# Shared expert in a two-layer block: tails of gate and up in one stationary block, a stacked down tail, and an earlier gather of the first rows

## What is computed

```
x = x + tanh(g_xattn[0]) * conv_attention(ctx, ctx, layernorm(x))        # the conv stage
x = x + tanh(g_ffn[0])   * moe(layernorm(x))                             # shared and routed experts
x = x + tanh(g_xattn[1]) * linear_attention(layernorm(x), ctx)
x = x + tanh(g_ffn[1])   * soft_moe(x)

def moe(x):
    topk_w, topk_idx = top_k(softmax(x @ router_w.T), 2)                 # weights sum to 1
    shared = (silu(x @ s_gate_w + s_gate_b) * (x @ s_up_w + s_up_b)) @ s_down_w + s_down_b
    return shared + sum over the chosen experts of weight * expert(x)
```

## Time and profile before

| what | us |
|---|---|
| median of three runs (1761.22 to 1765.13) | 1762.69 |
| the profiled execution | 1761.46 |
| its span, from the first to the last instruction | 1759.6 |
| PE busy in the span | 1572.1 (89%) |
| PE busy from 350 to 400 us, of 50 | 49.90 |
| mean granted clock of PE, as a share of 2.4 GHz | 0.954 |

### The profile page before, as it was taken

How to read it: one execution, slowest core, us unless ns; L and a number is a source line. 1 busy time by engine, 2 the same in 40 slices (tenths; PEclk the granted TensorE clock), 3 DMA queues, 4 the chain that set the end, 5 groups by cost and what they waited for, 6 DMA issues and landing times. The chain is left out here.

```text
span 1759.6 us, 27544 instructions
## 1 busy us (share of the span) xinstructions
PE 1572.1 (89%) x9484; PEld 913.1 (52%) x9484; DVE 1091.7 (62%) x2221; ACT 756.3 (43%) x1392; POOL 512.9 (29%) x428
## 2 busy tenths in 40 slices
PE   4989948999799999879888887889999999999997
PEld 3778833444356566435344443545555555555554
DVE  7998845335623343368586874766676767575663
ACT  5443214333123333234343452656564656566462
POOL 0657824333324444234342331120202010111101
PEclk7999979999999999889899998989999999999998
DMA  9545544745596898552425226624160505142241
GB/s 208 140 118 155 161 143 137 202 145 154 169 213 177 220 221 198 206 197 84 144 84 168 66 77 239 199 61 92 41 132 6 125 18 113 41 90 60 61 91 42
DMA packets 293579, 228.83 MB, mean 130 GB/s; under 512 B 197778, under 2 KB 241298, under 8 KB 291170
## 3 DMA queue, kind: packets, MB, share of 16 engines
q1 hardware_dynamic: 244912, 156.73, 34.7%
q10 hardware_dynamic: 39298, 40.54, 7.9%
q0 software_dynamic: 9264, 30.15, 5.6%
HBM read 125.58 MB, written 54.87 MB: 103 GB/s over the span
## 5 line engine op out<-in xcount | busy, mean ns | idle before, releaser
L2136 POOL TENSOR_TENSOR s_h_lo<-s_h,s_h_hi 128x512 f16<-128x512 f32 x32 | 36.9, 1154 | 552.8 <-DVE s_h_hi L2338 552.8
L1275 DVE TENSOR_TENSOR e_h<-e_up,e_silu 128x352 f32<-128x352 f32 x39 | 20.4, 524 | 138.7 <-ACT e_silu L1220 123.5
L2356 PE MATMUL s_ring<-w_mu,s_xt_hi 128*128 128x512 f16 x256 | 98.5, 385 | 5.9 <-DMA w_mu<-mu_split 2.8
L2264 DVE TENSOR_REDUCE s_top<-s_lg 128x1 f32<-128x512 f32 x64 | 43.9, 686 | 93.4 <-ACT s_lg L2178 93.2
L2357 PE MATMUL s_ring<-w_mu,s_xt_hi 128*128 128x512 f16 x256 | 98.5, 385 | 0.0
L2358 PE MATMUL s_ring<-w_mu,s_xt_lo 128*128 128x512 f16 x256 | 98.2, 384 | 0.0
L2356 PE MATMUL s_acc<-w_w,s_g_hi 128*128 128x512 f16 x256 | 97.1, 379 | 0.1
L524 PE MATMUL ring<-prod_hi,toep 128*128 128x288 f16 x320 | 92.8, 290 | 4.9 <-DVE terms L438 4.7
L2356 PE MATMUL s_ring<-w_w,s_xt_hi 128*128 128x512 f16 x256 | 97.0, 379 | 0.0
L2357 PE MATMUL s_ring<-w_w,s_xt_hi 128*128 128x512 f16 x256 | 97.0, 379 | 0.0
L2358 PE MATMUL s_ring<-w_w,s_xt_lo 128*128 128x512 f16 x256 | 97.0, 379 | 0.0
(11 more groups left out here) (387 smaller groups left out, 4793.7 us busy)
## 6 DMA issues: line engine op xcount, KB each, us to landing
expert_rows<-e_y SPq DMA_DIRECT2D x39, 256.0 KB
a_part_in<-in_L_ffn_W ACTq DMA_DIRECT2D x32, 256.0 KB
w_split<-a_part_q ACTq DMA_DIRECT2D x32, 256.0 KB
w_w<-w_split SPq DMA_DIRECT2D x8, 1024.0 KB, 21.6
toep<-ssm_split ACTq DMA_DIRECT2D x14, 512.0 KB, 5.3
stage<-in_L_ffn_gate_w SPq DMA_DIRECT2D x8, 704.0 KB
stage<-in_L_ffn_up_w SPq DMA_DIRECT2D x8, 704.0 KB
xattn_w_split<-e_part_q ACTq DMA_DIRECT2D x20, 256.0 KB
```

The lines of the kernel that those rows point to most:

```text
L2264: V.tensor_reduce(top[:, t, j:j + 1], lg[:, t, j * D:(j + 1) * D], AX.X, ALU.max).then_inc(S["top_done"], 1)
L2356: mm(out_, a[0], b_[0], start=first, stop=False)
```

## The change

- In the conv stage the normalised rows live in `rows_ahead` instead of `xq`. Ahead of the last store, when all earlier stores have landed, SP gathers partitions 0 to 119 of chunk 0's x1 rows from DRAM into `rows_ahead`; behind the store it copies the last 8 partitions from `gated`, in four transfers, and the block's end waits for them. The first normalisation reads `rows_ahead`; the load of chunk 0's x1 into the shared phase stays, for the residual, but stands behind the up pieces.
- The host gives gate without its last 64 columns, and in front of up a block of 128: the last 64 of gate, the last 64 of up. One block of 12 matmuls then gives gate's tail on partitions 0 to 63 and up's on 64 to 127 of one bank. Silu reads the lower half and writes the upper, and h of the tail stands on the upper half.
- The last 64 rows of down are loaded twice, to both halves of the partitions. POOL writes the tail's `h_lo` to the lower half of `h_hi`'s tail. One matmul over 128 rows then makes hi*hi + lo*hi, a second over the upper 64 rows hi*lo.
- The two up pieces have homes of their own (the buffer of silu and h, and the one of `xq`), so that four pieces are issued without a wait. ACT and DVE split the gate pieces ahead of the turned rows, the up pieces after them.

```diff
@@ conv_stage, SP
             for s in range(STEPS):
+                if s == STEPS - 1:
+                    sp.wait_ge(turned["q"], 8)
+                    for u in range(2):
+                        sp.wait_ge(stored[u], (STEPS - 1 - u) // 2 * 16 + (0 if u else 16))
+                    first = P - SSM_I
+                    sp.dma_start(k.ahead.home[0:first, :, :], x1_rows[0:first]).then_inc(k.ahead.x1_loaded, 16)
                 store(s)
+                if s == STEPS - 1:
+                    for t in range(4):
+                        sp.dma_start(k.ahead.home[first:P, t, :], gated[t:P:2 * B, s % 2, :]).then_inc(k.ahead.x1_last, 16)
...
+            sp.wait_ge(k.ahead.x1_last, 4 * 16)
@@ shared_phase, SP
-            load_x(0, 0)
...
             for n, piece in enumerate(pieces):
-                if n >= 2:
-                    sp.wait_ge(sw_lo, n + 1)
-                sp.dma_start(staged(piece, n % 2), piece[2]).then_inc(stage_loaded[n % 2], 16)
+                if n == 4:
+                    load_x(0, 0)
+                if n >= 4:
+                    sp.wait_ge(sw_lo, n - 1 if n < 6 else n + 1)
+                if n == NP - 1:
+                    for half in (LOW, HIGH):
+                        sp.dma_start(staged(piece, n)[half], piece[2]).then_inc(piece_loaded(n)[0], 16)
+                    continue
+                sp.dma_start(staged(piece, n), piece[2]).then_inc(piece_loaded(n)[0], 16)
@@ ACT (DVE likewise with rest_of_turned)
-            split_turned(0)
             for n, piece in enumerate(pieces):
+                if n == 2:
+                    split_turned(0)
@@ POOL
-                    nc.gpsimd.tensor_tensor(h_lo[0:r, m, :], h[0:r, u, :], h_hi[0:r, m, :], ALU.subtract).then_inc(h_lo_done, 1)
+                    nc.gpsimd.tensor_tensor((h_lo[:, m, :] if m < SK - 1 else h_hi[LOW, m, :]), h[r, u, :], h_hi[r, m, :], ALU.subtract).then_inc(h_lo_done, 1)
@@ PE
-                    for o, (hi, lo) in enumerate(((sg_hi, sg_lo), (su_hi, su_lo))):
+                    for o, (hi, lo, at) in enumerate((gate_, up_) if m < SK - 1 else (both,)):
+                        cols = slice(at, at + P)
...
-                        nc.tensor.matmul(tr[:, t, :], h_hi[0:r, m, tok], sd_hi[0:r, m, :], start=(m == 0), stop=False)
-                        nc.tensor.matmul(tr[:, t, :], h_hi[0:r, m, tok], sd_lo[0:r, m, :], start=False, stop=False)
-                        last = nc.tensor.matmul(tr[:, t, :], h_lo[0:r, m, tok], sd_hi[0:r, m, :], start=False, stop=(m == SK - 1))
+                        nc.tensor.matmul(tr[:, t, :], h_hi[:, m, tok], sd_hi[:, m, :], start=(m == 0), stop=False)
+                        last = nc.tensor.matmul(tr[:, t, :], h_hi[r, m, tok], sd_lo[r, m, :], start=False, stop=(m == SK - 1))
+                        if m < SK - 1:
+                            nc.tensor.matmul(tr[:, t, :], h_lo[:, m, tok], sd_hi[:, m, :], start=False, stop=False)
```

More of the change, by code:

```diff
@@ L151, in conv_stage @@
         rows = {"c": sb("c_rows", [P, B, D]), "q": sb("x_rows", [P, B, D])}
-        xn = sb("xq", [P, 4, D])
+        xn = k.ahead.home
         ssm, d_col = sb("ssm", [SSM_H, PAD]), sb("d_col", [SSM_H, 1])
@@ L583, in shared_phase @@
         taken[0] = 6656
-        sg_hi, sg_lo = (lent(KD * I_SH).rearrange("p (k i) -> p k i", k=KD) for _ in range(2))
+        sg_hi, sg_lo = (lent(KD * WHOLE).rearrange("p (k i) -> p k i", k=KD) for _ in range(2))
+        taken[0] = 6656 + 2 * KD * I_SH
         xt = lent(2 * KD * CH).rearrange("p (k i) -> p k i", k=2 * KD)
@@ L626, in shared_phase @@
         stage_loaded = [sem(f"stage_loaded{u}") for u in range(2)]
+        up_loaded = [sem(f"up_loaded{u}") for u in range(2)]
         x_loaded = [sem(f"x1_loaded{u}") for u in range(2)]
@@ L650, in shared_phase, with staged, piece_loaded @@
             e = min(b + 2, whole)
-            pieces.append((sd_hi[:, b:e, :], sd_lo[:, b:e, :], s_down[b * P:e * P, :].rearrange("(k p) n -> p k n", p=P), P))
+            pieces.append((sd_hi[:, b:e, :], sd_lo[:, b:e, :], s_down[b * P:e * P, :].rearrange("(k p) n -> p k n", p=P), slice(0, P)))
         rest_rows = I_SH - whole * P
-        pieces.append((sd_hi[0:rest_rows, whole:SK, :], sd_lo[0:rest_rows, whole:SK, :],
-                       s_down[whole * P:I_SH, :].rearrange("(k p) n -> p k n", k=1), rest_rows))
+        tail_rows = slice(0, P)
+        pieces.append((sd_hi[tail_rows, whole:SK, :], sd_lo[tail_rows, whole:SK, :],
+                       s_down[whole * P:I_SH, :].rearrange("(k p) n -> p k n", k=1), tail_rows))
         NP = len(pieces)
         assert NP % 2 == 0
-        def staged(piece, u):
+        def staged(piece, n):
             hi, _, _, rows = piece
-            k_, n = hi.shape[1], hi.shape[2]
-            return stage[0:rows, u, 0:k_ * n].rearrange("p (k n) -> p k n", n=n)
+            k_, cols = hi.shape[1], hi.shape[2]
+            home_ = {2: gated[:, :, :].rearrange("p a i -> p (a i)"), 3: xq.rearrange("p t q d -> p (t q d)").bitcast(F32)}.get(n, stage[:, n % 2, :])
+            return home_[rows, 0:k_ * cols].rearrange("p (k n) -> p k n", n=cols)
+        def piece_loaded(n):
+            return (up_loaded[n % 2], 16) if n in (2, 3) else (stage_loaded[n % 2], (n // 2 + (n < 2) + (n >= NP - 1 and n % 2)) * 16)
         def expert_weights(n):
@@ L759, in _ @@
                 for m in range(SK):
-                    r, u, n = rows_of(I_SH, m), m % 2, c * SK + m
+                    r, u, n = rows_at(m), m % 2, c * SK + m
+                    g = slice(0, r.stop - r.start)
                     act.wait_ge(gu_done, n + 1)
@@ L826, in normalise @@
             def normalise(c, u):
-                dve.wait_ge(x_loaded[u], (c // 2 + 1) * 16)
-                ln.statistics(nc, dve, x_in[u], c)
+                rows_ = x_in[u] if c else k.ahead.home
+                if c:
+                    dve.wait_ge(x_loaded[u], (c // 2 + 1) * 16)
+                else:
+                    dve.wait_ge(k.ahead.x1_loaded, 16)
+                    dve.wait_ge(k.ahead.x1_last, 4 * 16)
+                ln.statistics(nc, dve, rows_, c)
                 if c == 1:
@@ L2479, in transformer @@
         k.gates, k.tanh_gates = sb("gates", [P, 4]), sb("tanh_gates", [P, 4])
+        sb, _, sem = opener(nc, whole)
+        k.ahead = RowsAhead(sb, sem)
         down_whole, down_tail = scratch("down_whole", (P, 2, E, 2 * D), F16), scratch("down_tail", (I_MOE - 2 * P, 2, E, D), F16)
@@ L2483, in transformer @@
                    a[F + "down_w"], down_whole, down_tail)
-        sb, _, sem = opener(nc, whole)
-        k.ahead = RowsAhead(sb, sem)
         with ExitStack() as routed:
@@ L2538 @@
         a[new] = columns(a.pop(old))
+    F, whole = "L0_ffn_s_", I_SH // P * P
+    gate, up = a[F + "gate_w"], a[F + "up_w"]
+    a[F + "gate_w"] = gate[:, :whole]
+    a[F + "up_w"] = np.concatenate([gate[:, whole:], up[:, whole:], up[:, :whole]], axis=1)
+    a["s_up_b_cols"][P // 2:, SK - 1] = a["s_up_b_cols"][:P // 2, SK - 1]
     a["L1_ffn_mu"] = a["L1_ffn_mu"].reshape(D, ES)
```

54 lines of the change are left out of this document (34 added, 20 removed).

## The result

The changed kernel took 1747.62 us (median of four executions, 1746.63 to 1749.83) against 1762.76 for the kernel before on the same chip: 15.1 us less, a ratio of 0.9923 (95% interval 0.9905 to 0.9940). The forecast was 22.8 us less. The sign held, and the time lies inside the stated range (1735 to 1749), but outside the forecast's own 1736.5 to 1744: a third of the gain did not come.

A forecast was written before the change was run, and what follows sets the result against it. Bounds: a load-and-split chain at the shared expert's head, PE in the middle, DVE in the last chunk. Gains 13.5 + 0.4 + 7.1 + 1.8 = 22.8 us off 1761.46 gave 1738.7, median 1740, range 1735 to 1749.

The forecast's parts named there:

- (a): End of conv stage: early gather and four copies delay the shared phase's first load by 1.5 us, bounds 0 to 3.6.
- T: Time of SP's first load of the shared phase, 240.70 before; forecast 1.5 us later.
- (b): Head of the shared phase: new load and split order brings S 15.0 us nearer to T.
- S: Time of SP's first load of expert weights, 280.25 before (T + 39.6); forecast T + 24.6.
- chunk 0: Shared phase's first chunk, hanging on S: 0.4 us left of the shorter down product, the transposes taking the rest.
- (c): Gate and up tails in one block: 12 matmuls fewer per chunk, 2.6 us plus 0.1 for the width change.
- (d): Down product tails: two matmuls instead of three for each of four token tiles, 0.86 us a chunk.
- chunk 3: Last chunk of the shared phase: block 5's gain reaches DVE's gating product, which waited 1.82 us; 1.8 us gained.
- E: DVE's first expert product, 492.94 before; the prediction had what comes after 477 us untouched, moving as a whole.
- The chain of the head: Loads and splits of shared weights: PE's up half at T + 16.8, first expert load at T + 24.6.
- the slower rival: 64-row matmuls on the upper half stall PE at 32 changes; 1772 us at 1 us each; chance 0.03.
- the head gives only the early rows: Rival: queue holds up and down pieces back, S gains at most 6.9 less 1.5 us; time 1748; chance 0.13.

The follow-up runs named there:

- e11: The changed kernel itself, unaltered, run again on another chip for a second trace: median 1743.97 us, ratio 0.9930 to the kernel before.
- e8: Changed kernel, but all 128 partitions gathered from input x and the four copies left out; one run, no ratio, SP's first load at 243.14.
- e4: Changed kernel with chunk 0 reordered: POOL's fourth split behind the last h_lo, DVE's fourth row remainder behind block 5's gating product; ratio 0.9912 to the kernel before.
- e6: Changed kernel with PE's order changed in chunk 0's down product: blocks 0 to 3 of all token tiles first, then 4 and 5; ratio 0.9918 to the kernel before.
- e2: Changed kernel without early rows and with the head's old order, leaving only the matmul part: 1752.39 us, ratio 0.9949 to the kernel before.
- e1: Changed kernel without the early gather and copies, x1 loaded first in the shared phase: ratio 0.9922 to the kernel before.
- e3: Changed kernel with partitions 0 to 103 gathered ahead of store 14, the rest copied behind stores 14 and 15: ratio 0.9875 to the kernel before.
- e10: Changed kernel with rows gathered by step pairs, the copies' wait moved later, chunk 0's fourth POOL split and DVE remainder later: 1739.03 us, ratio 0.9892 to the kernel before.

## Why the prediction was too large, by its own steps

| step | forecast | measured |
|---|---|---|
| (a) T later | -1.5 | -6.0 |
| (b) S nearer to T | 15.0 | 14.2 |
| chunk 0 | 0.4 | -1.7 |
| (c), (d) in chunks 1 and 2 | 7.1 | 6.9 |
| chunk 3, to DVE's last operation | 1.8 | 1.5 |
| from there to E (e11: +0.7) | 0 | -0.8 |
| sum | 22.8 | 14.1 |

Each measured term is a difference of the marks above: (b) is 39.55 less 25.31, chunk 0 is 6.59 less the 8.28 by which S moved, and so on.

**The step that failed is (a)**, a term that was mis-sized: 1.5 us, bounded by 3.6, where the runs show 6.0. It had both of its parts and put them over each other: the copies as 0 to 3.6 us, and the gather, 2.6 us at 370 GB/s, which "may hold up the last store by as much; that is inside the same bounds". They are not beside each other. The store and the copies stand behind the gather in one queue, so the parts add. The gather held up the store by 4.5 us: 2.7 in the shape of e8, and 1.8 because the rate was read from transfers of 128 partitions and the one in question had 120. The copies cost 0.8, and 0.7 lie ahead of the store. That 2.6 and 3.6 make 6.2, near the 6.0, would have been luck: the gather costs more than its part and the copies less. The bounds should have taken a lower rate for a shape that no row showed. (The 2.0 us that the prediction names from the Trainium skill, DMA: Bandwidth & Descriptors, Anatomy of one DMA, stand there for transfers that POOL issues, and the copies are SP's.)

**Chunk 0 failed too**: 0.4 us forecast, 1.7 lost. I looked for what is next late among the transposes, rightly (S + 42.4 before, and e4 and e6 end on them), but not at POOL. Its split of the fourth expert piece stands between `h_lo` of blocks 3 and 4. Before, PE came to that point with waits of 1.1 and 0.7 us, and the granted clock stayed at 1.00. With 12 matmuls less in front it comes earlier and waits 3.5, and then works at half the clock. Either alone would have stayed hidden: without the waits (4.0) or without the half clock (3.0) PE would have been through by some S + 41 or S + 42 (estimates from the S + 44.6 of the changed kernel), ahead of the transposes at S + 42.3 (e6) to 43.1 (e4). Together they end 1.5 to 2.3 us behind them. e2 shows this without the rest of the change, e6 its full size.

**What held.** The chain of the head: its links came 0.2 to 1.4 us later than worked out (PE's up half at T + 17.5 for T + 16.8), and S at T + 25.3 for T + 24.6. (By its own terms, ACT's second gate piece should have stood at 9.0, not 9.2.) The pitch of the saved matmuls (3.45 of 3.55, in e2 as well). The 64-row matmuls on the upper half: PE passes from one to the next block in 0.31 us, as before, so the slower rival had no ground. The last chunk. Of the rivals, "the head gives only the early rows" named the right time (1748) for a wrong reason, by luck: the early rows gave little. Of the 14.2 us by which S is nearer to T, 11.1 are there without them (e1: 268.74 less 240.28 is 28.5, for 39.6 before), from the up pieces' own homes and the new order. The other 3.1 come from x1's load behind the pieces, which the early rows allow, and T pays 6.0 for it.

## What to carry to other kernels

A transfer put ahead of the last one in a queue delays what is behind it (here by 2.7 us for 1 MB, and by 4.5 in the odd shape), so add its time to theirs, and place it where the queue is empty; but look then at the background transfers of other engines there, as e3 did not. Where a stage ends with a wait for everything, a prefetch on its end can cost more than what it fetches early. After taking work off an engine, ask where it will now stand idle: a wait of 3.55 us was paid a second time in slower matmuls (3.0).

## What was not expected of the hardware

A transfer over 120 partitions moved at 213 to 223 GB/s with the engines' share at 0.96 to 1.01 (240 to 246 while it started, at 0.83), over 112 at 287 to 297, over 128 at 311 to 324, with rows of 2 KB in each case. After PE had stood idle for 3.55 us (changed kernel) and 4.71 us (e6), the granted clock was 0.50 for the next stretch of 4 us; after 2.56 us (e4) it was 1.00. And one of DVE's small operations on four columns, which takes 0.17 us where POOL is idle (e10, 296.06), took 1.71 while POOL split a piece (e4, 301.07).
